# Four-layer graph network: bias and residual of layer 2 moved to GpSimd, its softmax steps set between the units' operations

## What is computed

```python
h = (x @ W).reshape(n, H, C)                       # H = 8 heads, C = 32
a_src = jnp.einsum('nhc,hc->nh', h, att_src)
a_dst = jnp.einsum('nhc,hc->nh', h, att_dst)
e = a_src[src] + a_dst[dst]
e = jnp.where(e > 0, e, NEG_SLOPE * e)             # 0.2
m = jax.ops.segment_max(e, dst, num_segments=n)
ex = jnp.exp(e - m[dst])
alpha = ex / jax.ops.segment_sum(ex, dst, num_segments=n)[dst]
out = jax.ops.segment_sum(h[src] * alpha[..., None], dst, num_segments=n) + bias
y = out + x
y = (y - mu) / jnp.sqrt(var + EPS) * ln_w + ln_b
x = _layernorm(x + y)                              # the kernel's outer norm
```

## Time and profile before

| | us |
|---|---|
| median of 3 runs | 5425.84 (5420.32 to 5433.01) |
| the profiled execution | 5432.66 |
| its span in the trace | 5430.9 |
| PE / DVE / ACT / POOL busy | 4854.7 / 3946.8 / 2585.5 / 2142.3 |
| layer 1, from first GpSimd instruction to the next stage's first | 1226.1 to 2637.6 |
| layer 2 | 2637.6 to 3994.9 |
| last stage | 4648.0 to the end |

### The profile page before, as it was taken

One profiled execution on the slowest core, in us unless ns is written; L12 is line 12 of the kernel. 1 busy time (PEld: TensorE's weight loads), 2 busy tenths in 40 slices (PEclk: granted clock), 3 DMA queues, 4 the chain that ended last, 5 costly groups with the idle time before them and its releaser, 6 DMA issues. The chain is left out here.

```text
span 5430.9 us, 97954 instructions
## 1 busy us (share of the span) xinstructions
PE 4854.7 (89%) x22356; PEld 3728.2 (69%) x22356; DVE 3946.8 (73%) x13675; ACT 2585.5 (48%) x6082; POOL 2142.3 (39%) x2171
## 2 busy tenths in 40 slices
PE   6999877778999999999788888888879999788888
PEld 3666544447888888888577777777756666577777
DVE  4333399997888888888389999999965555566666
ACT  2333344444555555555355655655531111355555
POOL 4666400006555555555245555554445555000000
PEclk8999955559999999999799999999989999899999
DMA  4444399983444444444356666666545555567665
GB/s 113 133 133 133 106 291 295 288 266 106 131 135 130 130 135 131 131 134 130 118 164 186 190 185 181 195 179 184 174 136 163 163 164 164 175 214 214 212 207 167
DMA packets 893392, 921.21 MB, mean 170 GB/s; under 512 B 116765, under 2 KB 855444, under 8 KB 893126
## 3 DMA queue, kind: packets, MB, share of 16 engines
q1 hardware_dynamic: 484174, 444.55, 28.2%
q10 hardware_dynamic: 333688, 318.57, 17.2%
q0 software_dynamic: 75264, 155.06, 10.1%
HBM read 632.48 MB, written 337.88 MB: 179 GB/s over the span
## 5 line engine op out<-in xcount | busy, mean ns | idle before, releaser
L1175 POOL DMA_INDIRECT nodes_near_rows<-hh_d,source_row x392 | 397.9, 1015 | 605.0 <-DVE nodes_weighted L1348 529.1
L767 PE MATMUL nodes_agg<-nodes_msg,nodes_hot 128*128 128x264 f32 x784 | 410.0, 678 | 135.8 <-issue 92.6
L846 POOL DMA_INDIRECT nodes_near_rows<-x_d,nodes_cur x392 | 425.7, 1086 | 236.3 <-POOL nodes_cur L841 169.2
L1491 POOL DMA_INDIRECT edges_xg<-x_d,edge_rows x392 | 371.5, 948 | 258.6 <-PE edges_x_ps L1517 176.2
L432 POOL DMA_INDIRECT edges_xg<-in_x,edge_rows x392 | 370.5, 945 | 256.3 <-PE edges_t_ps L448 135.0
L767 PEld LDWEIGHTS nodes_agg<-nodes_msg,nodes_hot 128*128 128x128 f32 x784 | 229.2, 323 | 316.2 <-issue 275.2
L649 ACT ACTIVATE nodes_x<-nodes_outer_rows,nodes_outer_shift,nodes_outer_rstd 128x256 f32<-128x256 f32 x784 | 425.6, 593 | 19.6 <-DVE nodes_outer_shift L642 14.4
L1733 PE MATMUL nodes_agg<-w_s,nodes_xT 128*128 128x256 f32 x1568 | 412.2, 386 | 1.9 <-ACT nodes_xT L1750 1.9
L854 POOL TENSOR_TENSOR nodes_xb<-nodes_xin,row_L_gnn_b 128x512 f32<-128x512 f32 x196 | 248.1, 1266 | 380.6 <-DVE nodes_inner_rows L880 380.4
L959 PE MATMUL nodes_h_ps<-w_h,nodes_x2T 128*128 128x272 f32 x1568 | 392.2, 393 | 6.7 <-ACT nodes_x2T L1036 6.7
L969 PE MATMUL nodes_hid_ps<-nodes_zT,w_a 128*128 128x256 f32 x1568 | 372.4, 381 | 0.7 <-ACT nodes_zT L1045 0.7
(11 more groups left out here) (209 smaller groups left out, 12468.5 us busy)
## 6 DMA issues: line engine op xcount, KB each, us to landing
nodes_xin<-x_d SPq DMA_DIRECT2D x588, 256.0 KB, 3.1
nodes_msg<-msg_d SPq DMA_DIRECT2D x784, 132.0 KB, 3.5
x_d<-nodes_x ACTq DMA_DIRECT2D x392, 256.0 KB, 3.2
hh_d<-nodes_hh ACTq DMA_DIRECT2D x196, 264.0 KB
x_d<-nodes_y ACTq DMA_DIRECT2D x196, 256.0 KB
nodes_hin<-hh_d SPq DMA_DIRECT2D x196, 256.0 KB, 3.8
nodes_xin<-in_x SPq DMA_DIRECT2D x195, 256.0 KB
out<-nodes_y ACTq DMA_DIRECT2D x195, 256.0 KB, 3.2
```

The lines of the kernel that those rows point to most:

```text
L767: last = nc.tensor.matmul(agg[ring(u, 2)][:, h, 0:D + H], hot[:, ring(u, 4), h, :], msg[:, r, h, :], start=True, stop=True)
L846: gp.indirect_dma_start(out=near_rows[:, r, h, :], out_offset=None, in_=x1_d, in_offset=bass.IndirectOffsetOnAxis(ap=cur[:, r, h:h + 1], a ...
L1175: gp.indirect_dma_start(out=near_rows[:, u % NR, h, :], out_offset=None, in_=hh_d, in_offset=bass.IndirectOffsetOnAxis(ap=source_row[:, 2 ...
L1491: gp.indirect_dma_start(out=xg[:, c % 8, k, :], out_offset=None, in_=x3_d, in_offset=bass.IndirectOffsetOnAxis(ap=edge_rows[:, c, k:k + 1] ...
```

## The change

It has five parts.

1. Layer 1 forms `x2b` = x2 + ln_b on GpSimd (lag 11) and stores that in the place of x2, at lag 13 instead of 11, by ScalarE's queue. `prepare` subtracts ln_b from the bias of layer 2's sum.
2. Layer 2: GpSimd adds this `xin` to the own message in place (lag 16, after VectorE's lag 15); TensorE's two matmuls of xin by the identity per unit go, and its sum waits for GpSimd (`based`). `xb` goes; VectorE's outer rows add xin itself. `xin` has ten slots and is loaded at lag 14; `own` and `weighted` have four slots.
3. The softmax steps of a group are spread over VectorE's step: a piece is marked, and the next waits (`settle`) only when its turn comes, after operations of the units.
4. The attributes' transposes, product, copy and store come 12 steps later (`LATER`), with loads to match; the first steps turn and copy only the one-hot half. `near_rows` is cleared slot by slot by VectorE in its first 16 steps.
5. Last stage: the edge lists are loaded by GpSimd's queue instead of ScalarE's.

```diff
+    def marked(eng, sem):
+        count = [0]
+        def mark(ins):
+            count[0] += 1
+            ins.then_inc(sem, 1)
+        def settle():
+            eng.wait_ge(sem, count[0])
+        return mark, settle
...
 # prepare, VectorE
+                link(nc.vector.tensor_tensor(b3[:, 0:D], b3[:, 0:D], rows["L2_gnn_ln_b"][0:3, :], ALU.subtract))
...
 # nodes1, GpSimd
+                    u = at(11)
+                    if u:
+                        gp.wait_ge(outer["normed"], num(u) + 1)
+                        if had(u, 4):
+                            gp.wait_ge(x2_out[ring(u, 4)], turn(u, 4) * 16)
+                        gp.tensor_tensor(x2b[:, ring(u, 4), :, :], x2[:, ring(u, 4), :, :], both(rows["L2_gnn_ln_b"]), ALU.add)\
+                          .then_inc(x2_biased, 1)
...
 # nodes1, ScalarE
-                            act.wait_ge(x2_out[ring(u, 4)], turn(u, 4) * 16)
+                            act.wait_ge(x2_biased, num(u) - 3)
...
-                        act.wait_ge(outer["normed"], num(u) + 1)
-                        act.dma_start(unit_rows(x2_d, u), x2[:, ring(u, 4), :, :]).then_inc(x2_out[ring(u, 4)], 16)
...
                     u = at(13)
                     if u:
+                        act.wait_ge(x2_biased, num(u) + 1)
+                        act.dma_start(unit_rows(x2_d, u), x2b[:, ring(u, 4), :, :]).then_inc(x2_out[ring(u, 4)], 16)
...
 # nodes2
-        NR, HR, WR = 16, 6, 3
+        NR, HR, XR, WR, HOT, LATER = 16, 6, 10, 4, 18, 12
...
 # nodes2, GpSimd
-                gp.memset(near_rows[:, :, :, :], 0.0).then_inc(zeroed, 1)
...
-                    u = at(18)
-                    if u is not None:
-                        gp.wait_ge(x_in[u % HR], u // HR * 16 + 16)
-                        if u >= WR:
-                            gp.wait_ge(outer["filled"], u - WR + 1)
-                        gp.tensor_tensor(xb[:, u % WR, :, :], xin[:, u % HR, :, :], both(rows["L2_gnn_ln_b"]), ALU.add)\
-                          .then_inc(biased, 1)
+                    u = at(16)
+                    if u is not None:
+                        gp.wait_ge(own_done, u + 1)
+                        gp.wait_ge(x_in[u % XR], u // XR * 16 + 16)
+                        gp.tensor_tensor(own[:, u % WR, :, :], own[:, u % WR, :, :], xin[:, u % XR, :, :], ALU.add).then_inc(based, 1)
...
 # nodes2, SyncE: the attributes' load moves from at(0) to at(12), beside hin; xin from at(12) to at(14)
+                        if u >= 4:
+                            sp.wait_ge(both_turned, u - 3 + LATER)
...
+                    u = at(14)
+                    if u is not None:
+                        if u >= XR:
+                            sp.wait_ge(outer["filled"], u - XR + 1)
...
-                    u = at(5)
+                    u = at(5 + LATER)
...
 # nodes2, TensorE
-                    u = at(2)
+                    u, e, k = at(2), at(2 + LATER), s - 2
...
-                        pe.wait_ge(x_in[u % HR], u // HR * 16 + 16)
                         pe.wait_ge(weighed, u + 1)
-                        pe.wait_ge(own_done, u + 1)
+                        pe.wait_ge(based, u + 1)
...
-                            nc.tensor.matmul(cols, ident[:, :], xin[:, u % HR, h, :], start=False, stop=False)
...
 # nodes2, VectorE: one of the pieces, the second of the shares
+                    g = shares
+                    if g is not None:
+                        n = of_group(g) * H
+                        settle()
+                        mark(nc.vector.tensor_tensor_scan(sm["total"][0:n, ::-1], sm["join"][0:n, 1:P + 1][:, ::-1], sm["run"][0:n, ::-1], -BIG,
+                                                          ALU.add, ALU.max))
...
+                    if s < NR:
+                        nc.vector.memset(near_rows[:, s, :, :], 0.0).then_inc(zeroed, 1)
...
 # nodes3
+            @blk.gpsimd
+            def _(gp):
+                for g in range(GROUPS_OF_UNITS):
+                    load_pairs(gp, sm, g)
...
-                    g = at(0)
-                    if g is not None and g % GU == 0:
-                        load_pairs(act, sm, g // GU)
```

258 lines of the change are left out of this document (155 added, 103 removed).

## The result

| | us |
|---|---|
| forecast | 5286 (5220 to 5395) |
| the change, median of 4 runs | 5363.14 (5362.33 to 5372.53) |
| before, median of 4 runs | 5423.08 (5416.23 to 5433.01) |
| ratio, 95% interval | 0.9892 [0.9872, 0.9912] |
| span of the profiled execution, after / before | 5360.6 / 5430.9 |

What follows compares the result with a forecast made beforehand. It took TensorE as the limit in layer 1 and the last stage, VectorE as leading in layer 2. Terms -38 - 68 - 12 - 28 + 6 = -140 from 5432.66 gave 5293, forecast 5286 after allowing for run median; range 5220 to 5395.

Steps and rivals of the forecast that it cites:

- Start of layer 2, -38: Layer 2's start: piecewise clearing and the later attribute product bring first weighted rows sooner, -38 us (-28 to -42).
- Ordinary units: Layer 2 units without softmax: TensorE falls from 5.31 to 4.44 us, below VectorE's 4.73; GpSimd's new wait priced at 0.
- Group steps, -68: Layer 2 steps with softmax: spreading the pieces cuts a group from 51.6 to 48.8 us, -68 (-22 to -150).
- body: Layer 2, VectorE's ordinary unit work in a group of eight: 8 x 4.73 us.
- exponential: Layer 2: the first sum scan, now early in its step, waits for ScalarE's exponential, 0.9 us a group.
- The rival that moving pays nothing there (5354): Layer 2 group steps: new holds and waits equal the old, so the 68 us are not gained; 5354, chance 20%.
- Holds: Layer 2: GpSimd's addition delays VectorE's keep, leaky score and backward scans until it ends, 5.0 us a group.
- The rival without holds: Layer 2: second softmax pieces slip in before GpSimd's addition; group 43.8 us, gain 190 for 68, 5164; chance 8%.
- End of layer 2, -12: After the gathers end, the addition no longer delays VectorE's shifts (1.24 us each instead of 0.15): -12 (-4 to -20).
- Last stage, -28: Last stage: list loads on GpSimd end TensorE's waits for the scores and copies, -28 us (-12 to -36).
- The rival of the clock: Layer 2: TensorE, with less to do, falls to the half clock more often; +41 for -68, 5395; chance 7%.
- the slower rival: Layer 1: both GpSimd additions hold VectorE's gamma products for their length, 235 us in place of 6, 5515; chance 6%.

Runs made afterwards that it cites:

- e8: Changed kernel with layer 2's attribute loads, transposes, product and store 12 steps earlier again, as before the change: 5400.6 us.
- e4: Changed kernel with all pieces of a group's softmax at the end of VectorE's step, in the old order: 5350.7 us.
- e1: Changed kernel with TensorE's transposes of a group's scores moved to the front of its step in layer 2: 5293.1 us.
- e11: Changed kernel with the last stage's shares' transpose behind the unit's sum and its edge lists issued by ScalarE again: 5294.5 us.
- e7: Changed kernel with TensorE's transpose of a group's shares behind the unit's sum in the last stage: 5269.5 us.
- e2: Changed kernel with the last stage's edge lists issued by ScalarE again, as before the change: 5369.6 us.

## Why the forecast was wrong

The sign was right and the range held the result, but the size was more than twice the measured. By its own steps:

- **Start of layer 2, -38: right** (-37.5). The scores were formed at 2667.9, 25.0 us after the stage's start for the 24.4 forecast, and the chain behind them took 15.0, the upper end of its range. Of the two parts of the change, e8 shows that without the later product 35.5 of it are lost; the other part was not run by itself.
- **Ordinary units: right in mechanism.** TensorE's two matmuls went, and VectorE's 4.73 is 4.63 where nothing disturbs. The addition's wait is hidden, as priced: no row of the trace shows TensorE waiting for it.
- **Group steps, -68: the step that failed.** The forecast said of the scan for the maxima and its wait for TensorE's score transposes: price 0, since the held leaky score gives TensorE time. That looks at when the scores are ready and not at when TensorE comes to turn them. The order of its step (work for the attributes and the one-hots first, scores behind) puts them 3.96 us in, and the two engines start their steps within 0.5 us of each other: 3.3 a group. That pairing could be read from the order and from TensorE's timeline of before. By terms, forecast against measured a group: body 37.8 / 37.0, pieces 5.1 / 4.8, holds 5.0 / 3.2, exponential 0.9 / 0.9, scores 0 / 3.3, and a remainder 0 / 1.5: 48.8 / 50.7. The remainder lies mostly in the first and the last step of the table above; that late copies of ScalarE and the half clock make it is argued, not shown. The rival that moving pays nothing there (5354) came nearest in time, and e4 bears it out for the placing of the pieces; e1 shows that one block on TensorE makes 70 us of difference.
- **Holds: mechanism right, sized too high.** 3.2 a group for 5.0, since the wait for the scores shielded the scan of the maxima (1.3) and the scan of the sums was held 0.5 for about 1.0; e1 brings the sum to 4.5. The rival without holds, with the rule of the Trainium skill (SBUF — State Buffer, Who interferes with whom) that who issues first goes ahead, did not come. The comparison of the masks starts ahead of the addition, while the second gather is under way (timelines of GpSimd and VectorE after the change), and is held to its end all the same:

```profile
2997.70 1.00 POOL L1195 DMA_INDIRECT nodes_near_rows<-hh_d,source_row  x1 [0.31 <-issue]
2998.73 1.27 POOL L1202 TENSOR_TENSOR nodes_own<-nodes_own,nodes_xin 128x512 f32<-128x512 f32 x1
```

```profile
2998.30 1.86 DVE L1391 TENSOR_TENSOR nodes_keep<-nodes_target 128x127 f32<-128x127 f32 x1
```

- **End of layer 2, -12: right in mechanism, but most of it did not reach the time.** The ordinary steps without gathers take 4.34 us for 5.40. Behind the last message product that gives -3.3. The last 16 steps before it take 99 us for 98 all the same, since the steps of the maxima among them take 11.5 and 9.4 us; with the pieces at the end of the step (e4) they take 83.
- **Last stage, -28: the term is right, its cover was not seen.** e11 measures 25 in the whole time and 31 in the stage. In the changed kernel the half clock behind the unchanged idle time of 2.39 us took most of it back. The rival of the clock was looked for in layer 2, at a price of 109 us; it came as 0.88 for 0.93 there and 0.95 for 0.99 in the last stage. The Trainium skill's warning on descriptors from GpSimd beside a fast VectorE (SBUF — State Buffer, Summary: rules for kernel authors) did not come true in this stage: each list load took GpSimd 484 ns in the middle, 570 at most.
- **Layer 1, +6: right in size** (+3.9), partly by luck. VectorE's idle time is down to 12 of 1200 us, so the next thing added there will count nearly in full. The forecast had one hold of about 1.3 us by x2b and put xb beside the statistics, released by VectorE's own sum. The runs show both additions in the products with gamma and beta, as the slower rival had it, but for 1.23 us a unit together and not 2.54; the rival decides from 1.34.
- Of the signs named: first product at 40.0, share at 0.41, no wait for scores in the last stage, layer 1 at its pace were met; VectorE at 95% and 6.1 us a unit failed (89%, 6.3), and it points to the wait; of the pieces named at 1 to 2 us the two backward scans took 0.41 and 0.87.

## What to carry to other kernels

When a step moves from the end of an engine's body to its front, price it by where its input is made in the producer's body: the difference of the two places, with both bodies started together, is the wait, whatever the input's own inputs are doing. Here, moving the pieces or the addition alone only changed which operation was held (the shares, then masks and scores, then the one-hots), until the addition and its victims were placed together; look for what runs in every unit first. And a stall that a change does not touch (2.39 us for the shares) may be worth more than the change: e7 gives 94 us with one block moved.

## What the runs showed of the hardware

- Behind the same idle time of 2.39 us TensorE's clock stayed at 1.00 in 17 of 22 groups before and in 2 of 22 after, and with the lists back on ScalarE in 12 of 22 (judged by the shares' step, 5.1 or above 6 us). What decides it was not found.
- Layer 2 with the very same code took 1223.7 (e2), 1232.1 (the change), 1237.5 (e11) and 1241.8 us (e7) from first to last message product, 18 us apart, so in this kernel a term of that size is read from its stage, not from the whole.
- The one-hots, a comparison of one SBUF operand with a scalar and its result in SBUF, are held by GpSimd's addition (439 ns in the mean for 280), not only operations with two SBUF operands. The Trainium skill (SBUF — State Buffer, Who interferes with whom) counts this kind among those that can take both port pairs; the trace agrees. It shows in before too: from 2760 to 3700, all 26 one-hots that took over 0.6 us ran beside the old addition, the longest 2055 ns (below, the tile hot in before, min/median/max ns). The statistics beside the same addition kept their 0.41.

```profile
L1306 DVE TENSOR_SCALAR nodes_hot<-iota,target_rel x392: 258/278/2055, 2644.8 to 3883.9; 128x128 f32<-128x128 f32 x196
```
